# Issuing the four row-fetch DMAs from GpSimd's queue instead of SyncE's, in an embedding, recurrence and feed-forward kernel

## The reference

```python
h = nan_to_num(take(embed_table, x), nan=0)
# recurrence over the 256 tokens of each sequence, on layernorm(h)
log_f, log_i = log_sigmoid(xn @ Wf.T), log_sigmoid(xn @ Wi.T)
log_h~ = log_g(xn @ Wh.T)
h = h + exp(scan(...))          # state_t = forget_t * state_(t-1) + input_t * candidate_t, from 0.5
# feed-forward, on layernorm(h)
a = bitlinear(xn, w_fc) + gate * (xn @ v.T @ fast_b.T @ u.T)
h = h + bitlinear(maximum(a, 0) ** 2, w_proj)
```

## Time and profile before

| | |
|---|---|
| median of three runs | 964.39 us (963.3 to 968.18) |
| the profiled execution | 965.65 us, its span 963.6 us |
| PE busy | 896.2 us, 93% of the span |
| ACT busy | 785.1 us, 81% |
| DVE busy | 747.0 us, 78% |
| POOL busy | 430.5 us, 45% |
| DMA engines, mean busy share | 30.2% for SP's queue, 2.0% for POOL's |

### The profile page before, as it was taken

How to read it: one execution, slowest core, us unless ns; L and a number is a source line. 1 busy time by engine, 2 the same in 40 slices (tenths; PEclk the granted TensorE clock), 3 DMA queues, 4 the chain that set the end, 5 groups by cost and what they waited for, 6 DMA issues and landing times.

```text
span 963.6 us, 17439 instructions
## 1 busy us (share of the span) xinstructions
PE 896.2 (93%) x5185; PEld 510.2 (53%) x5185; DVE 747.0 (78%) x1314; ACT 785.1 (81%) x1159; POOL 430.5 (45%) x459
## 2 busy tenths in 40 slices
PE   1566999999999999999999999999999999999976
PEld 1233555554555555555555555555555555555544
DVE  6667788787788887877788878878888787888653
ACT  3437789888888898888888988888889888888765
POOL 6532455444455544444555444445554544433120
PEclk9979999999999999999999999999999999999999
DMA  4222243324322333333233333332333333322320
GB/s 138 45 54 50 48 85 81 88 72 94 92 60 76 87 79 80 82 92 93 59 77 85 79 81 80 93 92 61 76 88 77 81 81 92 93 60 69 82 76 22
DMA packets 232410, 74.69 MB, mean 78 GB/s; under 512 B 206918, under 2 KB 226960, under 8 KB 232384
## 3 DMA queue, kind: packets, MB, share of 16 engines
q1 hardware_dynamic: 226240, 70.16, 30.2%
q0 software_dynamic: 6144, 4.21, 2.0%
HBM read 28.20 MB, written 25.17 MB: 55 GB/s over the span
## 4 chain that ended last, share of the span: by engine, by line
DMA 19%; DVE 19%; issue 15%; PE 13%; ACT 12%; SPq 10%; POOL 9%; ACTq 1%; DVEq 0%; POOLq 0%
DMA hid_rows<-spill 11%; SPq L290 9%; DMA spill<-hid_blocks 6%; POOL rstd L353 5%; PE bank L679 5%; ACT normed L418 5%; PE y_ps L653 4%; DVE stats L805 4%; DVE hid L1011 4%; POOL minus_mean L350 3%; PE bank L723 3%; DVE hid_blocks L1018 2%; DVE cand L992 2%; DVE h L1077 2%; ACT cand_lin L456 2%
## 5 line engine op out<-in xcount | busy, mean ns | idle before, releaser
L723 PE MATMUL bank<-x_cols,fc_t 128*128 128x512 f16 x1024 | 265.6, 382 | 0.7 <-issue 0.7
L679 PE MATMUL bank<-x_cols,w_hi 128*128 128x512 f16 x768 | 232.1, 384 | 32.6 <-DMA x_cols<-x_rows 30.8
L348 POOL TENSOR_SCALAR var_eps<-moments 128x4 f32<-128x4 f32 x64 | 61.3, 959 | 414.0 <-DVE moments L809 413.9
L679 PE MATMUL bank<-x_cols,w_lo 128*128 128x512 f16 x768 | 231.1, 383 | 0.0
L653 PE MATMUL y_ps<-proj_t,sq_hi 128*128 128x256 bf16 x1024 | 225.5, 273 | 3.7 <-DVE sq_lo L956 3.5
L653 PE MATMUL y_ps<-proj_t,sq_lo 128*128 128x256 bf16 x1024 | 225.5, 273 | 0.0
L338 POOL DMA_INDIRECT rows_raw<-table,idx_now x128 | 154.0, 1203 | 59.5 <-issue 31.0
L465 ACT ACTIVATE relu<-bank,relu_scale 128x512 f32<-128x512 f32 x256 | 165.5, 687 | 14.0 <-PE bank L727 14.0
L418 ACT ACTIVATE normed<-h,shift,rstd 128x256 f32<-128x256 f32 x256 | 132.7, 596 | 44.2 <-POOL shift L356 44.1
L723 PEld LDWEIGHTS bank<-x_cols,fc_t 128*128 128x128 bf16 x1024 | 100.7, 98 | 115.4 <-issue 3.8
L956 DVE TENSOR_TENSOR sq_lo<-sq,sq_hi 128x1024 f16<-128x1024 f32 x128 | 150.3, 1214 | 11.2 <-ACT sq L478 11.1
(11 more groups left out here) (133 smaller groups left out, 938.1 us busy)
## 6 DMA issues: line engine op xcount, KB each, us to landing
out<-out_sb SPq DMA_DIRECT2D x32, 512.0 KB, 3.0
spill<-hid_blocks SPq DMA_DIRECT2D x32, 256.0 KB, 2.0
hid_rows<-spill SPq DMA_DIRECT2D x128, 64.0 KB
rows_raw<-table,idx_now POOLq DMA_INDIRECT x128, 2.7
x_cols<-x_rows SPq DMA_TRANSPOSE x128, 2.8
sq<-w_fc SPq DMA_DIRECT2D x1, 1024.0 KB, 7.3
pj_raw<-w_proj SPq DMA_DIRECT2D x1, 1024.0 KB, 9.5
w_raw<-wf SPq DMA_DIRECT2D x1, 256.0 KB, 2.9
```

What stands on the lines that cost most here:

```text
L679: ins = pe.matmul(bank[gate_bank[p]][:, :], w[:, k, q, :], x_part(0, par, part)[:, :, k, :], start=(k == 0 and w is w_hi and part == 0), s ...
L723: pe.matmul(dst[:, :], fc_t[:, k, f * P:(f + 1) * P], x_part(1, 0, part)[:, :, k, :], start=(k == 0 and part == 0), stop=False)
```

## The change

`fetch_rows` moves from SP's program to POOL's, with its two waits. On SP the step becomes: transposes, spill, transposes, store. On POOL the four DMAs stand in steps 2 to 31 behind the gathers of chunk n+3 (from step 29 on there is nothing left to gather). In step 0 they stand behind the gathers and the small root of the low-rank scale, ahead of `root(1, 0)`. In step 1 they stand behind `root(0, 2)`, which is last there. The access patterns, the buffers and the semaphores stay as they are.

```diff
@@ sync: fetch_rows(c, par) and its call in step are taken out @@
-            def fetch_rows(c, par):
-
-                sp.wait_ge(blocks_spilled, 16 * (c + 1))
-                wait(sp, h1_low, c)
-                pass_on(sp, sp_passed, c)
-                rows = spill.rearrange("(i t) (j q c) -> i t j q c", t=BLOCK, j=TILES, q=B)
-                for i in range(B):
-                    sp.dma_start(hid_rows[:, :, BLOCK * i:BLOCK * (i + 1)],
-                                 rows[i].rearrange("t j q c -> q t j c")).then_inc(blocks_moved[par], 16)
...
                     spill_blocks(n)
-                    fetch_rows(n, par)
@@ gpsimd @@
+            def fetch_rows(c, par):
+
+                pool.wait_ge(blocks_spilled, 16 * (c + 1))
+                wait(pool, h1_low, c)
+                pass_on(pool, pool_passed, c)
+                rows = spill.rearrange("(i t) (j q c) -> i t j q c", t=BLOCK, j=TILES, q=B)
+                for i in range(B):
+                    pool.dma_start(hid_rows[:, :, BLOCK * i:BLOCK * (i + 1)],
+                                 rows[i].rearrange("t j q c -> q t j c")).then_inc(blocks_moved[par], 16)
...
                     pool.tensor_tensor(a_norm[:, :], a_ss[:, :], plus_half[:, :], ALU.pow).then_inc(a_rooted, 1)
+                    fetch_rows(0, 0)
                     root(1, 0)
...
                 if first:
                     root(0, 2)
+                if not start and known_below(n, N):
+                    fetch_rows(n, par)
```

## The result

The changed kernel takes 1136.78 us (median of 5 runs, 1134.38 to 1141.3), the kernel before beside it 966.48 us. The ratio is 1.1771 with a 95% interval of 1.1735 to 1.1806: **slower by 17.7%**, some 170 us. The forecast was 1098 us with a range of 968 to 1375 us.

The account below looks back on a forecast made before the run. Bound: a latency loop of 27.57 us a step, 0.21 us above PE's work. The profiled 965.65 us plus 130 (31 steps of 4.2) plus 4 for chunk 1, less 1.3 and rounded, gave 1098 us; range 968 to 1375.

Parts of the forecast that it names:

- the cap: Most a shorter loop can give back before PE binds: 0.21 us a step, 6 us over 31 steps.
- POOL in time, nothing queued behind the wait that matters: POOL's gathers end just as the spill lands, and later POOL work can wait; queue ahead of the fetch costed at 0.
- The pitch of the issues: Time p from one POOL fetch issue to the next: 2.3 us, bounds 1.3 and 5.2; four issues take 4p - 0.3.
- The tail: From the last issue's end to DVE's release: 2.3 us, the gather's 1.7 plus half a 1.28 us transfer.
- X: Growth of the loop per step from the longer fetch, 11.2 us instead of 7.0: 4.2 us.
- What the change takes from SP: Four issues, 4.34 us a step, leave SP; the transposes behind may start up to 4 us earlier; effect costed at 0.
- Chunk 1: Its fetch stands behind `root(0, 2)` and lands 6.6 us late, partly beside PE's long projection; 4 us taken.
- PE's clock: PE idling some 4 us a step might lower its clock; left out of the sum, on the range's upper side.
- Cheap issue: Rival: POOL issues a fetch DMA at the gather's pitch, 1.30 us, giving 972 us; chance 0.20.
- the costly one: Rival: POOL's issue time goes with the number of pieces, pitch 4.3 us, giving 1350 us; chance 0.27.
- Faster: Rival: POOL's pitch below the break-even of 1.25 us shortens the loop until PE binds, giving 958 us; chance 0.06.
- The two rules of the Trainium skill: Many descriptors cost little extra, pitch near 1.30 us; DVE's guard blocks POOL up to 0.67 us a step, 21 us.

Follow-up runs that it names:

- experiment 3: Kernel before, fetch still on SP, cut into one DMA for each 32 partitions instead of each 32 columns: 956.56 us, ratio 0.9911 to the kernel before.
- experiment 2: Changed kernel, fetch on POOL, cut into one DMA for each 32 partitions instead of each 32 columns: 958.94 us, ratio 0.9935 to the kernel before.
- experiment 5: Changed kernel, each fetch DMA reading 128 pieces of 512 bytes instead of 512 of 128, outermost still 4, result rows not turned: 971.1 us, ratio 1.0078.
- experiment 6: Changed kernel with only SP's 512 KB store held until the fetch has landed, transposes going at once: 1097.44 us, ratio 1.1419 to the kernel before.
- experiment 1: Changed kernel with SP's next transposes and the store behind them held until the fetch has landed: 1202.83 us, ratio 1.2462 to the kernel before.
- experiment 7: Changed kernel with the fetch of chunk 1 issued ahead of `root(0, 2)` in step 1: 1131.77 us, ratio 1.1759 to the kernel before.

## Why the prediction was right, and which terms were off

- **The bound.** Right. A loop of latencies, 0.21 us above PE's work, with the fetch in it: what the fetch gained in length (5.3 us) came back in the step (5.8 us), and experiment 3 took the loop below PE's work and won 9 to 10 us, where the cap said 6.
- **POOL in time, nothing queued behind the wait that matters.** Right for the gathers, which end at 622.54 us, just ahead of the landing. But I took 0 for the start, and POOL needed 0.6 us from the landing to its first issue.
- **The pitch of the issues.** Forecast 2.3 us, between 1.3 and 5.2; measured 1.60 us, with no gap. The split by the smallest POOL instruction put it too high, and the earlier trace rows was misread for it: 0.96 us is not what the smallest takes. POOL's L356, on as many numbers, takes 335 ns (mean) in the kernel before:

```profile
L356 POOL TENSOR_TENSOR shift<-minus_mean,rstd 128x4 f32<-128x4 f32 x64 | 21.4, 335 | 5.0
```

  The 512 pieces in total do not set the pitch, as experiment 2 shows; the pieces for each DMA engine fit it and experiment 5. 4p - 0.3 came out as 6.4 instead of 8.9 us.
- **The tail.** This is the term that was mis-sized most: forecast 2.3 us from the end of the last issue to the release, measured 635.26 - (628.38 + 1.57) = 5.3 us. The gather's tail was a poor stand-in, as it moves fewer and longer pieces. About 1.2 to 1.6 us of it is contention (experiments 6 and 1). The rest belongs to POOL's DMAs of this cut by themselves. Experiment 1 shows it in a fetch whose first issue started at 549.96 us and whose last DMA landed at 560.3 us, with nothing of SP beside it (columns as in the earlier trace rows):

```profile
549.96:552.20 2.24, 2.24 (x12) 1.05 (x11) 1.81 (x2) 1.90 (x3) 2.24 (x2) 1.00 0.00 0
552.30:554.50 2.20, 2.20 (x12) 0.99 (x11) 2.17 (x4) 2.17 (x3) 2.20 (x2) 1.00 0.52 37
554.50:560.20 5.70, 4.67 (x24) 2.21 (x22) 0.76 (x1) 5.70 (x9) 1.83 (x2) 1.00 0.59 36
```

  Nothing moved for the first 2.2 us, and then 37 GB/s at most. At that rate the 65.5 KB of one DMA take 1.8 us or more, which is longer than the 1.6 us of an issue. The prediction had carried over SP's 51 GB/s, hence 1.28 us, and said that from POOL the transfers are faster than the issues. That step failed.
- **The errors cancelled in part.** -2.5 us for the issues, +3.0 for the tail, +0.6 for the start: 11.2 + 1.1 = 12.3 us. That X = 4.2 came out as 5.3 and the forecast near is thus partly luck: the two terms were each off by more than half of X.
- **"What the change takes from SP" at 0.** This step failed. I had looked at who waits for SP's transposes and store, and not at what they would collide with. The transposes start 0.7 us after the spill's issue instead of 6.8 us, which is 6 us sooner and not 4, as the wait for the spill's landing is gone too; the store starts 5 us sooner. The store alone cost 34 to 39 us (experiment 6).
- **Chunk 1.** Forecast 4 us, 4.0 us by the trace; the times cannot confirm it (experiment 7).
- **PE's clock.** Forecast near 1.00, with a fall on the upper side. It was 0.92 in the steady stretch, and 0.73 in a projection that followed a wait, which then took 9.65 us instead of 7.0. PE had idled 4.1 us before it, and from 607.4 to 607.6 us the granted clock was 0.50, the 1.2 GHz level; from 617.25 us on it was 1.00, the 2.4 GHz level. It stays almost hidden: DVE waited for the projection in at most 12 of 23 steps, 7.3 us in total, 0.3 us a step. With the 5.4 us by which the way from the spill's issue to the add grew (14.5 - 9.1, the spill's own 0.3 us in it), this is 5.7 of the 5.8 us. I had also put PE's idle time at gate product 4; it stands at the projection, behind `sq_lo`.
- **The rivals.** "Cheap issue" was nearer for the instruction than the costly one, but it had the same tail, which was wrong. "Faster" needed a pitch under 1.25 us, which experiment 2 reached by another cut.
- **The two rules of the Trainium skill** (page "DMA: Bandwidth & Descriptors" and page "SBUF — State Buffer", the sections that the prediction names). That many descriptors can be emitted before their cost shows: not here, the fetch's instruction took 0.9 us more with the cut by columns than in experiment 5. That a two-port `tensor_scalar` of DVE and GpSimd block each other: the trace agrees, but mostly it was DVE that lost. The guard, first before, then after (min/median/max in ns):

```profile
L793 DVE TENSOR_SCALAR rows_fin<-rows_raw x32: 658/668/693, 16.4 to 864.0; 128x1024 f32<-128x1024 f32 x32
```
```profile
L795 DVE TENSOR_SCALAR rows_fin<-rows_raw x32: 660/1270/1708, 15.2 to 1027.7; 128x1024 f32<-128x1024 f32 x32
```

DVE had nothing else to do there, so it cost nothing. Three of POOL's 128 issues took longer than 1.75 us, up to 2.05, and each of them overlapped a guard.

What stays open: why a DMA from POOL with this cut moves nothing for 2.2 us after the start of its issue and then only 37 GB/s, where SP had 51 with the same pieces. That the count of DMA engines is what the other cut changes was argued and fits two experiments; no run counted the engines. Two of the four DMAs issued from SP and two from POOL were not tried.

## What to carry to other kernels

Before moving a DMA to another queue, ask what its own shape costs: with the outermost dimension of both sides at 32, and not 4 on one side, the same pieces took about half the issuing time from either queue, and the choice of queue was worth some 2 us by the medians and not 170. When a loop of latencies sets the step, the price of a queue is the time from the awaited landing to the release, issues and tail together, and one row of another kind of DMA does not give the tail. And a queue that is freed starts its next DMAs earlier: look up what they will run beside.

## What the hardware showed that I had not expected

- The cut by partitions, with 32 outermost instead of 4, nearly halved the duration of the issuing instruction: 1.59 to 0.84 us on POOL, 1.16 to 0.64 us on SP (medians).
- A DMA of 512 pieces from POOL took 4.5 us at best to land; by the other cut it was 2.3 us.
- From POOL the pieces travel bundled. Packets of the hardware and the software queue, before:

```profile
q1 hardware_dynamic: 226240, 70.16, 30.2%
q0 software_dynamic: 6144, 4.21, 2.0%
```

and after:

```profile
q1 hardware_dynamic: 160192, 61.77, 24.5%
q0 software_dynamic: 16384, 13.39, 12.5%
```

66048 packets from SP became 10240 from POOL, 80 for a DMA of 512 pieces. It did not make them faster. The last number is the time that the packets took, as a share of 16 engines' span. In experiment 1, where nothing of SP ran beside the fetch, and for POOL's queue in experiment 2:

```profile
q1 hardware_dynamic: 160192, 61.77, 19.5%
q0 software_dynamic: 16384, 13.39, 13.6%
```
```profile
q0 software_dynamic: 10240, 12.60, 6.7%
```

  From SP the 128 DMAs of the fetch thus took 0.302 x 963.6 - 0.195 x 1201.3 = 57 us of all 16 engines. From POOL they took 0.136 x 1201.3 - 0.020 x 963.6 = 144 us with the same cut, and 0.067 x 960.6 - 19 = 45 us with the cut by partitions. The count of packets is not the reason: experiment 5 has 16384 on that queue as well, and is fast.
